# Attention, latent attention and a mixture of experts on one Trainium2 core: scores as two passes on row halves, outputs divided in the routing phase

## The reference

```
xn = layernorm(x)
attn = softmax(rope(xn Wq + bq) . rope(xn Wk + bk)) (xn Wv + bv)     # the phase 4 and GpSimd blocks: heads against heads, per row
h = rmsnorm(xn) * g1;  q = h Wq;  c = h Wdkv;  k = c Wuk;  v = c Wuv
a = softmax(causal(q . k / sqrt(16)))                                # 16 heads, 2048 x 2048 each, 4 batches
x2 = xn + (a v) Wo
out = x + attn + x2 + sum over the top 2 of 8 experts of gate_e * silu(rmsnorm(x2) g2 w1_e) w2_e
```

## Time and profile before

| | us |
|---|---|
| median of 3 runs | 3378.97 |
| lowest, highest | 3376.55, 3382.85 |
| the profiled execution, own time | 3397.75 |
| its span, first to last instruction | 3396.2 |
| TensorE busy | 2743.9 |
| VectorE busy | 2474.5 |
| GpSimd busy | 2210.9 |
| ScalarE busy | 1561.3 |

### The profile page before, as it was taken

How to read it: one execution, slowest core, us unless ns; L and a number is a source line. 1 busy time by engine, 2 the same in 40 slices (tenths; PEclk the granted TensorE clock), 3 DMA queues, 4 the chain that set the end, 5 groups by cost and what they waited for, 6 DMA issues and landing times. The chain is left out here.

```text
span 3396.2 us, 56592 instructions
## 1 busy us (share of the span) xinstructions
PE 2743.9 (81%) x16988; PEld 1397.0 (41%) x17168; DVE 2474.5 (73%) x3932; ACT 1561.3 (46%) x2346; POOL 2210.9 (65%) x1179
## 2 busy tenths in 40 slices
PE   5959978998989898989899989977766988889700
PEld 2535532333333323332333333226655777777600
DVE  5538868877878797889778887714444999999444
ACT  2312235565656665666556666662222444444200
POOL 3423359678767966796669777964663666666476
PEclk9979999999999999999999999997767999999855
DMA  4995560443144214422442240016546666666676
GB/s 135 215 287 194 190 151 18 62 62 54 31 63 64 45 39 63 64 41 44 62 62 36 47 64 14 19 33 222 193 143 214 215 210 199 210 201 206 216 219 208
DMA packets 366323, 408.79 MB, mean 120 GB/s; under 512 B 66690, under 2 KB 310788, under 8 KB 366084
## 3 DMA queue, kind: packets, MB, share of 16 engines
q1 hardware_dynamic: 320132, 323.96, 39.2%
q0 software_dynamic: 17920, 54.55, 5.0%
q10 hardware_dynamic: 28032, 27.27, 2.3%
HBM read 256.12 MB, written 149.03 MB: 119 GB/s over the span
## 5 line engine op out<-in xcount | busy, mean ns | idle before, releaser
L885 DVE TENSOR_REDUCE p_piece_max<-p_ring 128x1 f32<-128x512 f32 (+3 forms) x2160 | 1319.0, 656 | 189.1 <-PE p_ring L1010 94.5
L959 ACT ACTIVATE p_probs<-p_st 128x1024 f32<-128x1024 f32 (+3 forms) x1280 | 1078.0, 894 | 682.5 <-PE p_st L1045 342.4
L827 POOL TENSOR_TENSOR p_terms<-p_head_p,p_head_in 128x4096 f32<-128x4096 f32 x32 | 347.7, 10865 | 314.4 <-ACT p_head_p L966 313.7
L1042 PE MATMUL p_st<-unit_q,unit_k 98*128 98x512 bf16 (+7 forms) x1642 | 433.7, 353 | 51.5 <-DMA unit_q<-p_neg_lo 31.5
L1057 PE MATMUL p_pv<-p_probs,unit_vg 128*32 128x512 f32 (+3 forms) x3520 | 409.6, 542 | 0.0
L1687 POOL TENSOR_TENSOR p_pv<-p_pr,p_qkv 128x4096 f32<-128x4096 f32 x32 | 347.8, 10868 | 38.6 <-ACT p_pr L1785 37.9
L1004 PE MATMUL p_ring<-unit_k,unit_q 64*128 64x512 bf16 (+3 forms) x1600 | 275.2, 358 | 75.0 <-DVE p_piece_max L885 74.5
L1858 PE MATMUL p_y_ps<-p_w,p_hid 128*128 128x256 f32 x1152 | 281.0, 400 | 31.6 <-ACT p_hid L1798 31.6
L812 POOL TENSOR_TENSOR p_terms<-p_head_in 128x4096 f32<-128x4096 f32 x32 | 282.0, 8814 | 4.9 <-POOL p_head_s L820 4.4
L1845 PE MATMUL p_hid_ps<-p_rT,p_w 128*128 128x256 f32 x1152 | 263.9, 382 | 4.8 <-issue 4.3
L833 POOL TENSOR_TENSOR p_terms<-p_terms 128x2048 f32<-128x2048 f32 (+2 forms) x96 | 252.6, 2632 | 17.1 <-POOL p_terms L833 11.4
(11 more groups left out here) (202 smaller groups left out, 3825.4 us busy)
## 6 DMA issues: line engine op xcount, KB each, us to landing
p_w<-ffn_w SPq DMA_DIRECT2D x144, 512.0 KB, 5.2
qk_parts<-p_parts SPq DMA_DIRECT2D x64, 384.0 KB, 3.3
head_qkv<-p_heads SPq DMA_DIRECT2D x16, 1536.0 KB, 6.2
p_rows<-sorted_rows SPq DMA_DIRECT2D x72, 256.0 KB, 4.5
expert_rows<-p_y ACTq DMA_DIRECT2D x72, 256.0 KB, 5.8
unit_q<-qk_parts SPq DMA_DIRECT2D x132, 128.0 KB, 10.3
unit_k<-qk_parts SPq DMA_DIRECT2D x132, 128.0 KB, 10.8
p_x<-attn_x SPq DMA_DIRECT2D x32, 512.0 KB, 5.2
```

Of the source, the lines that this page charges most:

```text
L827: step(nc.gpsimd.tensor_tensor(terms[:, :, :, :], head_p[:, u, :, :].unsqueeze(2).to_broadcast([P, H, DH, H]), head_in[:, u, 2, :, :].rear ...
L885: nc.vector.tensor_reduce(piece_max[:, h:h + heads, i, pc], ring_ps[bank][:, 0:heads * width].rearrange("p (h k) -> p h k", h=heads), AX_X ...
L959: nc.scalar.activation(probs[:, 2 * turn_of(s, i) + u, :, 0:width], st_ps[u][:, :, 0:width], ACT.Exp).then_inc(probs_done, 1)
L1042: last = nc.tensor.matmul(st_ps[u][:, j, 0:width], k6[s][0:rows, hh, kt * P:(kt + 1) * P], q6[s][0:rows, hh, c * CT + skip:(c + 1) * CT], ...
```

## The change

A unit's q6 and k6 are laid out anew: of each head the first four products stand in 64 rows and the other two with the maximum's two rows in 34 rows of another slot; heads 0 and 1 have rows 0 to 63, heads 2 and 3 rows 64 to 127. The scores of two heads are made by four matmuls, two passes on each half. A mask is added by two matmuls of 64 columns for each half. The turn and the division in phase 2 are gone: SP stores each head's 17 rows as they are, gathers a unit's sums in the next unit after the store of chunk 3, VectorE inverts them at step 10 (`INVERSE_AT`), SP stores the inverses. Phase 3 loads outputs and inverses (each inverse repeated over 16 rows), VectorE multiplies, and the transposes and copies of the outputs there are gone. Constant rows of ones come by DMA from a small tile; zero rows are not needed.

```diff
-MAX_ROWS = 4 * DH
-HALVES = (slice(0, PAIR), slice(PAIR, HG))
+HALF = 4 * DH
 ROWS = P
-NEG_ROW = (6 * DH, 2 * DH)
-SCORE_ROWS = (6 * DH + 2, P)
+NEG = 2 * DH
+PASS_ROWS = (HALF, NEG + 2)
+SUMS = DH + 1
...
+def half_rows(half, second):
+    return slice(half * HALF, half * HALF + PASS_ROWS[second])
...
+            row, second = half * HALF + g % 4 * DH, g // 4
+            slots = slice(second * PAIR, (second + 1) * PAIR)
+            sp.dma_start(q6[row:row + DH, slots, :], qk_heads[0, a, heads, :, :].rearrange("h d t -> d h t")).then_inc(loaded, 16)
+            sp.dma_start(k6[row:row + DH, slots, :], qk_heads[1, k, heads, :, :].rearrange("h d t -> d h t")).then_inc(loaded, 16)
...
+            row = half * HALF + NEG + r
+            sp.dma_start(q6[row:row + 1, PAIR:HG, :].rearrange("a h (i p) -> a (h i) p", p=P),
...
-def set_constant_rows(engine, eng, q6, k6, zeroed, ones_set, count, apart):
-    gap = slice(2 * DH, MAX_ROWS)
-    engine.memset(q6[gap, HALVES[1], :], 0.0)
-    engine.memset(k6[gap, HALVES[1], :], 0.0).then_inc(zeroed, 1)
-    wait_apart(eng, zeroed, count, apart)
-    for half, hs in enumerate(HALVES):
-        last = engine.memset(k6[NEG_ROW[half]:NEG_ROW[half] + 2, hs, :], 1.0)
-    last.then_inc(ones_set, 1)
+def set_ones(eng, k6, ones, stored):
+    for half in range(2):
+        row = half * HALF + NEG
+        for slot in range(PAIR, HG):
+            eng.dma_start(k6[row:row + 2, slot, :].rearrange("r (c t) -> r c t", c=NC),
+                          ones[0:2, :].unsqueeze(1).to_broadcast([2, NC, CT])).then_inc(stored, 16)
+def gather_sums(eng, sums, sums_of, n, loaded):
+    for hh in range(HG):
+        eng.dma_start(sums[hh * VW:(hh + 1) * VW, :], sums_of[n, hh, DH, :].rearrange("(q j) -> q j", q=VW)).then_inc(loaded, 16)
...
+def add_mask(nc, out, half, j, mask, ident_b):
+    rows = slice(half * HALF, (half + 1) * HALF)
+    return nc.tensor.matmul(out[:, j * HALF:(j + 1) * HALF], mask[rows, j + 1 - half, :], ident_b[rows, rows],
+                            start=False, stop=True, skip_group_check=True)
...
+    half, slot = h // PAIR, h % PAIR
+    rows = half_rows(half, 0)
+    last = nc.tensor.matmul(out[:, 0:width], q6[rows, slot, i * P:(i + 1) * P], k6[rows, slot, pc * CT:pc * CT + width],
+                            start=True, stop=pc != i // TT, skip_group_check=True)
+    if pc == i // TT:
+        for j in range(2):
+            last = add_mask(nc, out[:, width - P:width], half, j, mask_q, ident_b)
...
+            for _, k6_u, _ in units:
+                set_ones(sp, k6_u, ones, next_loaded)
...
-            for k, (uq, uk, _) in enumerate(units):
-                set_constant_rows(nc.vector, dve, uq, uk, gap_zeroed, ones_set, k + 1, apart)
...
+            def store_o(n, c):
+                wait_apart(sp, pv_copied, NC * n + c + 1, apart)
+                for hh in range(HG):
+                    sp.dma_start(sums_of[n, hh, :, c * CT:(c + 1) * CT],
+                                 pv_sb[hh * VW:hh * VW + SUMS, c % 2, :]).then_inc(o_stored[c % 2], 16)
+            def load_sums(n):
+                for slot in range(2):
+                    wait_apart(sp, o_stored[slot], N_STORE_O * (1 + NC // 2 * (n + 1)), apart)
+                wait_apart(sp, inverse_done, n + 1, apart)
+                gather_sums(sp, sums, sums_of, n, sums_loaded)
+            def store_inverse(n):
+                wait_apart(sp, inverse_done, 1 + n + 1, apart)
+                sp.dma_start(inverse_of[n].rearrange("h (q j) -> (h q) j", q=P // HG), inverse[:, :]).then_inc(inverse_stored, 16)
...
+            for n in range(UNITS):
+                s = n % SLOTS
+                if n + 2 < UNITS:
                     wait_apart(sp, pv_done, LAG + 1 + N_STEP * n, apart)
                     load(sp, n + 2, (s + 2) % SLOTS)
                 if n:
-                    store_o(n - 1, NC - 1, ring_item(n, s, 0)[0])
-                for c in range(NC - 1):
-                    store_o(n, c, ring_item(n, s, turn_item(c, has_next))[0])
-                if has_next:
+                    store_o(n - 1, NC - 1)
+                    load_sums(n - 1)
+                store_o(n, 0)
+                if n:
+                    store_inverse(n - 1)
+                store_o(n, 1)
+                store_o(n, 2)
+                if n + 1 < UNITS:
                     store_neg_rows(n + 1, (s + 1) % SLOTS)
-            for n in range(UNITS):
-                body(n, n % SLOTS, n + 2 < UNITS, n + 1 < UNITS)
-            store_o(UNITS - 1, NC - 1, N_ITEM * (UNITS - 1) + NC)
-            for s in range(2):
-                wait_apart(sp, o_stored[s], 16 * UNITS * NC // 2, apart)
+            store_o(UNITS - 1, NC - 1)
+            for slot in range(2):
+                wait_apart(sp, o_stored[slot], N_STORE_O * (1 + NC // 2 * UNITS), apart)
+            wait_apart(sp, inverse_stored, 16 * UNITS, apart)
...
-            set_constant_rows(nc.gpsimd, pool, q6[2], k6[2], gap_zeroed, ones_set, 1, apart)
-            wait_apart(pool, ones_set, 1, apart)
...
-            def divide(n, c, g, bank):
-                turned = ring_ps[bank][:, :].rearrange("p (t h v) -> p (t h) v", t=TT, h=HG)
-                dve.wait_ge(ring_filled, g + 1)
-                nc.vector.reciprocal(inv[:, c % 2, :], turned[:, :, DH]).then_inc(inv_done, 1)
-                dve.wait_ge(inv_done, 2 + NC * n + c + 1)
-                dve.wait_ge(o_stored[c % 2], 16 * (NC // 2 * n + c // 2))
-                nc.vector.tensor_tensor(o_sb[:, c % 2, :, :, :].rearrange("p t h d -> p (t h) d"), turned[:, :, 0:DH],
-                                        inv[:, c % 2, :].unsqueeze(2).to_broadcast([P, TT * HG, DH]), ALU.mult).then_inc(ring_free, 1)
+            def invert_sums(n):
+                dve.wait_ge(sums_loaded, N_STORE_O * (n + 1))
+                dve.wait_ge(inverse_stored, 16 * (n + 1))
+                nc.vector.reciprocal(inverse[:, :], sums[:, :]).then_inc(inverse_done, 1)
...
+                    if i == INVERSE_AT and not first(n):
+                        invert_sums(n - 1)
...
-                act.wait_ge(inv_done, NC * n + c + 1)
+                act.wait_ge(o_stored[c % 2], N_STORE_O * (1 + NC // 2 * n + c // 2))
...
-            def turn(n, c, g, bank):
-                pe.wait_ge(pv_copied, NC * n + c + 1)
-                pe.wait_ge(ring_free, g + 1)
-                for t in range(TT):
-                    last = nc.tensor.transpose(ring_ps[bank][:, t * P:(t + 1) * P], pv_sb[:, c % 2, t * P:(t + 1) * P], ident[:, :])
-                last.then_inc(ring_filled, 1)
...
+                for second in range(2):
+                    for half in range(2):
+                        rows = half_rows(half, second)
+                        last = nc.tensor.matmul(st_ps[u][:, half, 0:width], k6[s][rows, PAIR * second + u, kt * P:(kt + 1) * P],
+                                                q6[s][rows, PAIR * second + u, c * CT + skip:(c + 1) * CT], start=second == 0,
+                                                stop=second == 1 and not diagonal, skip_group_check=True)
+                if diagonal:
+                    for j in range(2):
+                        for half in range(2):
+                            last = add_mask(nc, st_ps[u][:, half, :], half, j, mask_k, ident_b)
...
-                sp.dma_start(o[:, c, :, :], o_v[b, c]).then_inc(loaded[c], 16)
+                for g in range(NG):
+                    k, rows = g // UNITS_K, slice(g % UNITS_K * HG * DH, (g % UNITS_K + 1) * HG * DH)
+                    sp.dma_start(oT[rows, c, k, :], o_v[b, c, g, :, 0:DH, :]).then_inc(loaded[c], 16)
+                for k in range(KD):
+                    sp.dma_start(inverse[:, c, k, :], inverse_v[b, c, k].unsqueeze(1).to_broadcast([UNITS_K * HG, DH, CT])).then_inc(loaded[c], 16)
...
+            def divide(b, c):
+                dve.wait_ge(loaded[c], N_LOADED * (b + 1))
+                nc.vector.tensor_tensor(oT[:, c, :, :], oT[:, c, :, :], inverse[:, c, :, :], ALU.mult).then_inc(divided, 1)
...
-            def copy_oT(n, s, projected):
-                for k in range(KD):
-                    act.wait_ge(oT_done, KD * n + k + 1)
-                    if projected:
-                        act.wait_ge(mla_done, 2 * n - 2)
-                    nc.scalar.copy(oT[:, s, k, :], oT_ps[k][:, :]).then_inc(oT_copied, 1)
...
-            def transpose_o(b, c, n):
-                pe.wait_ge(loaded[c], N_LOADED * (b + 1))
-                pe.wait_ge(oT_copied, KD * n)
-                for k in range(KD):
-                    for t in range(TT):
-                        last = nc.tensor.transpose(oT_ps[k][:, t * P:(t + 1) * P], o[:, c, t, k * P:(k + 1) * P], ident[:, :])
-                    last.then_inc(oT_done, 1)
...
```

207 lines of the change are left out of this document (89 added, 118 removed).

## The result

| | before | changed |
|---|---|---|
| median, us | 3380.91 (4 runs) | 3442.75 (4 runs) |
| lowest, highest | 3376.55, 3392.16 | 3439.03, 3446.91 |
| the profiled execution | 3397.75 | 3442.31 |
| its span | 3396.2 | 3440.8 |

The ratio is 1.0178, with a 95% interval of 1.015 to 1.0206. The changed kernel is slower by 62 us on the medians and by 44.6 us between the two profiled executions. The profiled execution of before stood 17 us above its median, that of the changed kernel at its own. Those 17 us can't be placed in the traces; the 44.6 can. The experiments further down ran in three groups, each with the kernel before beside it; its medians there were 3391 to 3393, so a comparison of times between groups is good to some 10 us, and I compare ratios there. Three experiments had one slow execution of 6468 to 11170 us; their medians count it, the ratios do not.

The account below looks back on a forecast made before the run. TensorE and VectorE were both taken as full in mid-unit, VectorE binding next; -20 + 2 + 12 + 1.5 - 16 + 16 - 10 - 3 + 4 = -13.5 gave 3384, 3366 on the median's scale, range 3260 to 3425.

Parts of the forecast that it names:

- 28.5 us after the trigger without a wait: Phase 2, first part of a unit: VectorE could reach step 10 at 28.5 us after the load's trigger (32.3 - 3.8).
- the gain of the changes of shape: TensorE in phase 2: about 0.10 us lost at each array shape change; 60 fewer in a unit's rest, 26 before it.
- -20 + 2 + 12 = -6 said: Start and phase 1: earlier first moments -20 us, DMAs for ones rows +2, shape changes between scores and projections +12.
- Rival D: Phase 2 scores: second passes' weight loads are exposed, 0.09 us each, unit 5.3 longer, kernel 3461; chance 0.1.
- Phase 3 is paced by GpSimd's scatters: Routing phase: scatters set the pace, VectorE's multiplication lies beside them, 23 loads before it cost more issue: +4 us (0 to 8).
- Sum of a unit: Phase 2, units 1 to 13: 115.5 us each against 114.3, +1.2 times 13, so +16.
- the 37.7: Phase 2, units 1 to 13: step 10, with the inversion waiting for the gathered sums, done 37.7 us after the load's trigger.
- The 2.0 for the half clock behind the wait: Phase 2: TensorE's clock at half after each stall for the sums costs 2.0 us a unit (0 to 4.2).
- rival C: Phase 2: sums land 2 us later (26) and half clock lasts twice as long (29), kernel 3421; chance 0.2.
- Unit 14: Phase 2, unit without a load: stores land at once, the inversion finds its sums, -3.8 - 6.1 = -10 us.
- Unit 15: Phase 2, last unit: no maxima to make, only turns and changes go, -3 us.
- rival B: Phase 2: the wait for sums binds little, unit 104.3 us, 146 less, kernel 3220, half of it 3293; chance 0.2.

Follow-up runs that it names:

- no_inverse_loads: The changed kernel without the loads of repeated inverses and without the multiplication in the routing phase, outputs left undivided: 3411.19 us, ratio 1.0052 to before.
- halves_alone: The kernel before with the new layout, passes, masks and ones rows; turn, division, stores of outputs and routing phase untouched: 3373.99 us, ratio 0.9945 to before.
- late_inversion: The changed kernel with the inversion of the sums at step 16 instead of 10: 3389.69 us, ratio 0.998 to before.
- late_load_by_4: The changed kernel with the gather ahead of the load, inversion at step 16, load in groups of four transfers: 3312.5 us, ratio 0.9736 to before.
- halves_load_by_4: halves_alone with the load behind the store of chunk 3, in groups of four transfers, each waiting for the one before: 3299.18 us, ratio 0.9714 to before.

## Why the prediction was wrong

Forecast 3366, faster; measured 3442.75, slower, beyond the range's end of 3425. Step by step:

**Right.** What row halves give until step 10 (28.5 us after the trigger without a wait; in unit 14, where no load is triggered, VectorE has it 32.2 us after the transpose, and the load of other units comes 3.7 or more after theirs: 32.2 - 3.7 = 28.5); that the inversion waits behind the load in units 1 to 13, and TensorE with it, with half the clock after; that this uses up the gain of the changes of shape; the start up to the first transpose, 20.1 saved for 20.5 said. That holds in its parts too: VectorE's normalisations run 22.2 us earlier than in before until 152 us (20 said), the first of all transposes, that of phase 1, comes 6.1 us earlier (-20 + 2 + 12 = -6 said), and unit 0 with the start of phase 2 gives 14.0 (14.5 said). Rival D, and with it the rule of the Trainium skill (TensorE: Matmul & The Clock Gate, Part 3, "What overlaps and what doesn't"), did not decide: eight score passes take 0.95 us, so the second pass's weight load is not exposed here, and the trace does not agree with the rule.

Of the 77 us between forecast and result, 32 are the routing phase, 17 the units 1 to 13, 9 the other units and the rest of the program, and 18 the scale (below). One slip of the sum: 60 changes at 0.10 are 6.0 and not 5.8, which changes nothing, as VectorE bounds the rest of the unit in the sum.

**The step that failed most** is "Phase 3 is paced by GpSimd's scatters [...] lie beside that [...] **+4** (0 to 8)". It was +36, +20.8 at the start and +15.3 in pace. I put the added loads beside the scatters because VectorE and TensorE had slack, and never asked it of DMA and of SP's queue, although the repeated inverses, 128 x 1024 floats a chunk, are 0.5 MB on 1.5. Taking the repeated inverses and their multiplication away takes 34 us back (no_inverse_loads), and it brings the time that SP's queue is held at issue from 161.5 to 72.9 us; before had 16.2. That the lateness belongs to the outputs' way is shown by halves_alone, where it is gone.

**A term mis-sized.** "Sum of a unit: 37.7 + 70.3 + 2.0 + 5.5 = 115.5", +16 for 13 units, was 116.9, +33. The part of the sum that was off is the 37.7: the inversion ends 40.1 us after the trigger on average, 2.4 later than said (39.2 in unit 8, where the stores of chunk 3 have landed 35.5 after the trigger and not 33.6). The load itself lands no later than in before, 31.8 and 32.0 us after its trigger on average, so the added time lies in the four stores and the gather behind it; what makes them slower was not tried. Everything behind it, 70.3 + 2.0 + 5.5 = 77.8 as said, took 76.8. The 2.0 for the half clock behind the wait does not show: from the inversion's end to the next transpose it is 72.6 us in units 1 to 13, and 73.4 in unit 14, which has no such wait. So of rival C the first half came, sums that land some 2 us later, and the second, a clock that costs more, did not; units of 118 on average were not reached. The two errors have opposite signs, so the sum stood nearer than its terms. Unit 14 gave 7.4 and not 10: behind the inversion it took 73.4 + 3.7 = 77.1 where 70.3 + 5.5 = 75.8 stood, and in before it had been 0.8 shorter than an average unit. Unit 15 gave nothing where 3 stood.

**Not among my cases.** The holes of TensorE for its code. In the changed kernel the wait for sums mostly covered them (its nine units with such a hole take 116.7 us on average, the four without 117.2), so they were not what made the forecast wrong; but they are why taking the wait away gave 2.0% and not the 4% that units of 106 would be. My rival B, a wait that does not bind, was worth 146 us in my sum; late_inversion is that case, and it gave 1.0178 - 0.998 = 2.0%, 67 us. With the code's wait gone too (late_load_by_4) it is 4.4%, 150 us: 10.0 us a unit (106.9 against 116.9) where rival B had 11.2, for a TensorE that always has its code.

**Scale.** 18 us between forecast and result come from the profiled execution of before, which stood over its median; my sum took that along in proportion, and the changed kernel's profiled execution stood at its median.

**What it comes to.** The row halves are worth 2.9% once the load is given out behind the store of chunk 3 and in groups (halves_load_by_4). The outputs' new way takes 1.9 us from each unit (106.9 against 108.8, 27 over phase 2) and costs some 38 in the routing phase (77.3 + 253.4 against 54.5 + 238.2), a loss of some 11 on balance. The times, 3312.5 against 3299.18 in separate groups of runs, with ratios whose intervals overlap, can't tell the two kernels apart. What was not tried is the outputs' way with a routing phase whose inverses need no loads of half a megabyte a chunk.

**Open.** That the 16 KB transfers are TensorE's is read from the count of its instructions between them and between the holes, and from where they end; no row names their engine. And the transfers themselves are hardly shorter with groups (median 1.57 us beside the load of halves_alone, 1.73 beside groups of eight, 1.38 beside groups of four, 1.0 to 1.1 elsewhere): so what is long in a hole lies ahead of the transfer's start, and no row shows it. Whether fewer transfers in flight or DMA engines that are not full take it away is open too. That before has no such holes because its TensorE goes through its code more slowly is argued, not tested. In the first 15 us of a unit the clock is at half for 6.9 us on average in the changed kernel and for 4.1 in before; that early fall was not tested by itself.

## What to carry to other kernels

Before an added wait is priced, list every queue that the data goes through and what is issued ahead of it: 26 transfers ahead brought the sums some 11 us later than VectorE was ready for them, and six steps of lateness or another order of issue took the wait away. When work is cut into more and shorter matmuls, look for holes whose releaser is "issue" while a big load runs, and try giving that load out in groups: four and eight transfers helped here, one at a time cost more than it gave. And where an engine is relieved in one phase by loads in another, price them against the DMA and the issuing queue there, not against the engines' slack.
